# Edge network of a graph kernel: tile sums in two TensorE banks, accumulator written by ScalarE

## What is computed

```
q_i = K_v[dst]
alpha = concat([q_i * K_v[src], q_i * K_E]) * scale
gate = sigmoid(_ln(alpha, ln_g[h], ln_b[h]))
m = concat([V_v[src], V_E])
m = (m @ Wu[h] + bu[h]) * gate
m = _leaky(_ln(m @ Wm[h] + bm[h], mln_g[h], mln_b[h]))
heads.append(segment_sum(m, dst, num_segments=n))
```

## Time and profile before

| what | value |
|---|---|
| median of 3 runs | 13212.4 us (13209.07 to 13218.26) |
| profiled execution | 13231.7 us, span 13229.9 us |
| PE busy | 9252.9 us (70%) |
| DVE busy | 8863.8 us (67%) |
| GpSimd busy | 8813.8 us (67%) |
| ACT busy | 5824.9 us (44%) |
| mean granted TensorE clock | 0.930 of 2.4 GHz |

### The profile page before, as it was taken

One profiled execution on the slowest core, in us unless ns is written; L12 is line 12 of the kernel. 1 busy time (PEld: TensorE's weight loads), 2 busy tenths in 40 slices (PEclk: granted clock), 3 DMA queues, 4 the chain that ended last, 5 costly groups with the idle time before them and its releaser, 6 DMA issues.

```text
span 13229.9 us, 180603 instructions
## 1 busy us (share of the span) xinstructions
PE 9252.9 (70%) x45190; PEld 6129.7 (46%) x45190; DVE 8863.8 (67%) x20382; ACT 5824.9 (44%) x11467; POOL 8813.8 (67%) x6219
## 2 busy tenths in 40 slices
PE   1344444444475888888888888888888888669997
PEld 0233333333223665666666665666666656323322
DVE  3233333333206888888888888888888888327896
ACT  0111111111102666666666666666666666006442
POOL 1588888888603888888888888888888888000000
PEclk9999999999997999989999899999999999889997
DMA  9766666666693443434343344344443343569663
GB/s 413 235 157 150 151 152 151 150 152 153 163 416 109 120 119 119 120 119 120 119 120 119 118 120 120 119 120 119 119 120 120 119 119 110 231 279 359 232 219 125
DMA packets 1232544, 2147.28 MB, mean 162 GB/s; under 512 B 345985, under 2 KB 768210, under 8 KB 1218579
## 3 DMA queue, kind: packets, MB, share of 16 engines
q1 hardware_dynamic: 838120, 1657.69, 36.7%
q0 software_dynamic: 390240, 484.27, 16.9%
q10 hardware_dynamic: 4048, 3.51, 0.1%
HBM read 1652.11 MB, written 492.84 MB: 162 GB/s over the span
## 4 chain that ended last, share of the span: by engine, by line
POOL 44%; issue 20%; PE 15%; DMA 8%; DVE 5%; ACT 3%; SPq 3%; POOLq 1%; DVEq 1%; another core or an unknown queue 0%; ACTq 0%; PEldq 0%
POOL arena L1362 22%; POOL adj L1401 14%; POOL arena L1414 6%; PE psum L1273 5%; DMA arena<-adj 4%; DMA adj<-put_val,put_idx 3%; SPq L1453 3%; PE psum L1318 2%; ACT arena L980 2%; POOL arena L1417 1%; PE psum L1131 1%; PE psum L1285 1%; PE psum L1196 1%; PE psum L1209 1%; PE psum L1186 1%
## 5 line engine op out<-in xcount | busy, mean ns | idle before, releaser
L1401 POOL DMA_INDIRECT adj<-put_val,put_idx x1616 | 2638.3, 1633 | 844.9 <-issue 478.1
L980 ACT ACTIVATE arena<-arena 128x128 f32<-128x128 f32 x6464 | 2657.6, 488 | 298.2 <-DVE arena L774 170.4
L1110 PE MATMUL psum<-ke,arena 64*128 64x256 f32 x3232 | 1451.8, 640 | 1883.2 <-DMA arena<-in_edge_t 1883.2
L1362 POOL DMA_INDIRECT arena<-table1q,idx_dst x1616 | 2249.3, 1392 | 492.6 <-issue 492.6
L1362 POOL DMA_INDIRECT arena<-table,idx_blk x1616 | 1903.5, 1178 | 431.5 <-issue 374.9
L1110 PEld LDWEIGHTS psum<-ke,arena 64*128 64x128 f32 x3232 | 1039.7, 329 | 2294.9 <-issue 2025.9
L1196 PEld LDWEIGHTS psum<-wm,arena 128*128 128x128 f32 x12928 | 1755.6, 203 | 608.0 <-issue 509.4
L986 ACT ACTIVATE arena<-psum,cols 128x512 f32<-128x512 f32 x1616 | 1250.0, 774 | 1710.8 <-PE psum L1178 1386.7
L1186 PE MATMUL psum<-arena,wvu 128*128 128x512 f32 x3232 | 1894.1, 671 | 83.0 <-DVE arena L703 60.2
L1209 PE MATMUL psum<-arena 128*128 128x128 f32 x6464 | 1113.3, 325 | 1119.7 <-DVE arena L730 1107.0
L1196 PE MATMUL psum<-wm,arena 128*128 128x64 f32 x12928 | 1798.2, 285 | 5.9 <-issue 4.6
(11 more groups left out here) (208 smaller groups left out, 11727.7 us busy)
## 6 DMA issues: line engine op xcount, KB each, us to landing
arena<-adj SPq DMA_DIRECT2D x192, 1568.0 KB, 12.5
arena<-adj SPq DMA_DIRECT2D x336, 896.0 KB, 4.7
kept_keys<-arena SPq DMA_DIRECT2D x404, 512.0 KB
arena<-kept_keys SPq DMA_DIRECT2D x404, 512.0 KB
adj<-arena SPq DMA_DIRECT2D x98, 1568.0 KB
arena<-in_edge_t SPq DMA_DIRECT2D x808, 128.0 KB
kept_hot<-arena SPq DMA_DIRECT2D x404, 256.0 KB
arena<-kept_hot SPq DMA_DIRECT2D x404, 256.0 KB
```

Of the source, the lines that this page charges most:

```text
L980: A.activation(to, at_, ACT.Identity, bias=shift[z][:, n:n + 1], scale=rstd[z][:, n:n + 1]).then_inc(normed, 1)
L1110: last = M.matmul(psum[:, 2 + 2 * z + j, t * H * D:(t + 1) * H * D], edge0[z][:, 2 * j + t, :], ke[D:P, :], start=True, stop=True)
L1362: K.indirect_dma_start(out=dst[:, t, :], out_offset=None, in_=table, in_offset=bass.IndirectOffsetOnAxis(ap=idx[:, t:t + 1], axis=0)).then ...
L1401: K.indirect_dma_start(out=adj, out_offset=bass.IndirectOffsetOnAxis(ap=put_idx[s][:, j:j + 1], axis=0), in_=put_val[s][:, j:j + 1], in_of ...
```

## The change

Four tiles of a group are now summed in the same pair of banks (0 and 1, one for each pair of heads). A matmul of zeros opens both banks, and each tile's sums are accumulated at the tile's offset from the group's first destination, which TensorE takes from registers (16 loaded once in four iterations, from a table `offs` made ahead of the stage). ScalarE then writes the group's 512 columns to `acc`: the first column with what is there already as bias, for each pair of heads, the other 511 as a plain copy, since the edges are sorted and nothing else has been written there yet. DVE's four additions and its register loads are gone. `acc` has 384 columns more for each pair of heads. The bias of `o_pair` is one matmul over both tiles, ahead of the wait for the gates. `turn_x` writes bank 7 in place of 0.

```diff
-NW = NP + WIN
+NW = NP + G * WIN
@@ DVE, ahead of the stage
+            link(V.tensor_tensor(offs.rearrange("p (n t) -> p n t", t=G), dst_t[0:1, :].rearrange("p (n t) -> p n t", t=G),
+                                 dst_t[0:1, :].rearrange("p (n t) -> p n t", t=G)[:, :, 0:1].to_broadcast([1, NG, G]),
+                                 ALU.subtract))
@@ DVE, sweep1
-                if now[4] and s == 0:
-                    held[:] = block_bases(DVE, i - 4)
-                regs = held[G * s:G * s + G]
-                def add(t):
-                    if now[4]:
-                        dve.wait_ge(sums1, 2 * (i - 4) + t // 2 + 1)
-                        add_tile(added1, i - 4, t, acc[:, :, bass.ds(regs[t], WIN)],
-                                 psum[:, 1 + 6 * (t // 2), (t % 2) * 2 * WIN:(t % 2 + 1) * 2 * WIN].rearrange(
-                                     "p (j w) -> p j w", j=2))
-                add(0)
-                add(1)
                 if now[1]:
                     gate_m(3)
-                add(2)
-                add(3)
@@ ScalarE, sweep1
+                if now[4] and s == 0:
+                    held[:] = group_bases(ACTE, i - 4)
-                    A.activation(xt[s][0:D].rearrange("p t n -> p (t n)"), psum[0:D, 0, :],
+                    A.activation(xt[s][0:D].rearrange("p t n -> p (t n)"), psum[0:D, 7, :],
                                  ACT.Copy).then_inc(xt_ready, 1)
                 if now[2]:
                     take_o(1)
-            steps(act, sweep1, NG, 4, 2)
+                if now[4]:
+                    act.wait_ge(sums1, 2 * (i - 3))
+                    after(act, added1, 3 * (i - 4))
+                    for half in range(2):
+                        own = acc[:, half, bass.ds(held[s], 1)]
+                        A.activation(own, psum[:, half, 0:1], ACT.Identity, bias=own).then_inc(added1, 1)
+                    A.activation(acc[:, :, 1:NW][:, :, bass.ds(held[s], G * WIN - 1)], psum[:, 0:2, 1:G * WIN],
+                                 ACT.Copy).then_inc(added1, 1)
+            held = []
+            steps(act, sweep1, NG, 8, 4)
@@ TensorE, sweep1
+                if now[4] and s == 0:
+                    held[:] = block_offsets(PE, i - 4)
                 def o_pair(j):
+                    after(pe, o_taken, 2 * (i - 2) + j)
+                    M.matmul(psum[:, 6, :], ones3[:, :], bm_parts[:, :], start=True, stop=False)
                     pe.wait_ge(gm_ready, H * (i - 1))
-                    after(pe, o_taken, 2 * (i - 2) + j)
                     for t in range(2):
                         at_ = t * H * D
                         for h in range(H):
-                            M.matmul(psum[:, 6, at_ + h * D:at_ + (h + 1) * D], gm[z][:, h, 2 * j + t, :],
-                                     wm[:, h, :], start=h == 0, stop=False)
-                        last = M.matmul(psum[:, 6, at_:at_ + H * D], ones3[:, :], bm_parts[:, :],
-                                        start=False, stop=True)
+                            last = M.matmul(psum[:, 6, at_ + h * D:at_ + (h + 1) * D], gm[z][:, h, 2 * j + t, :],
+                                            wm[:, h, :], start=False, stop=t * H + h == 2 * H - 1)
                     last.then_inc(o_done, 1)
+                def clear_sums():
+                    after(pe, added1, 3 * (i - 4))
+                    for half in range(2):
+                        M.matmul(psum[:, half, :], zero_row[0:1, :], zero_row[0:1, 0:1].to_broadcast([1, G * WIN]),
+                                 start=True, stop=False)
                 def sums(j):
                     pe.wait_ge(hot_in[z], 16 * (2 * (k - 1) + s // 2 + 1))
                     pe.wait_ge(msg_ready, i - 3)
-                    after(pe, added1, G * (i - 5) + 2 * j + 2)
                     for t in (2 * j, 2 * j + 1):
                         for half in range(2):
-                            at_ = (t % 2 * 2 + half) * WIN
-                            last = M.matmul(psum[:, 1 + 6 * j, at_:at_ + WIN],
+                            last = M.matmul(psum[:, half, bass.ds(held[G * s + t], WIN)],
                                             msg[z][:, t * H + 2 * half:t * H + 2 * half + 2, :].rearrange("p h d -> p (h d)"),
-                                            onehot[z][:, t, :], start=True, stop=True)
+                                            onehot[z][:, t, :], start=False, stop=t == G - 1)
                 if now[4]:
+                    clear_sums()
                     sums(0)
```

More of the change, by code:

```diff
@@ L25 @@
 PE = mybir.EngineType.PE
+ACTE = mybir.EngineType.Activation
 P = 128
@@ L141, in gnn @@
         vecs = sb("vecs", [D, 6])
-        bm_row = sb("bm_row", [1, H, D])
-        bm_rest = sb("bm_rest", [1, H, D])
-        bm_up = sb("bm_up", [1, H, D])
+        bm_row, bm_rest, bm_up = (acc[0:1, i // 2, NP + i % 2 * H * D:NP + (i % 2 + 1) * H * D].rearrange(
+            "p (h d) -> p h d", h=H) for i in range(3))
+        zero_row = sb("zero_row", [1, P], BF16)
         bm_part = [sb(f"bm_part{i}", [1, H * D], BF16) for i in range(3)]
-        bm_parts = sb("bm_parts", [3, H * D], BF16)
+        bm_parts = sb("bm_parts", [3, 2 * H * D], BF16)
         ones3 = sb("ones3", [3, P], BF16)
@@ L417, in halves_of, with group_bases, block_offsets @@
             return slice(half * HALF + i * CH_N, half * HALF + (i + 1) * CH_N)
-        def block_bases(engine, g):
-            return bases(engine, dst_t[0:1, bass.ds(g * G, U * G)])
+        def group_bases(engine, g):
+            first = dst_t[0:1, bass.ds(g * G, U * G)].rearrange("p (u t) -> p u t", t=G)[:, :, 0]
+            return bases(engine, first)
+        def block_offsets(engine, g):
+            _, regs = nc.values_load_multi_w_load_instructions(
+                offs[0:1, bass.ds(g * G, U * G)], engines=(engine,), min_val=0, max_val=(G - 1) * WIN,
+                skip_runtime_bounds_check_because="every node has an edge, so a tile begins at most a window on")
+            return regs
         @block.vector
@@ L486, in one_hot @@
                     iota_f[:, :].unsqueeze(1).to_broadcast([P, G, WIN]), ALU.is_equal)
-            def add_tile(added, g, t, at_, sums):
-                after(dve, added, g * G + t)
-                V.tensor_tensor(at_, at_, sums, ALU.add).then_inc(added, 1)
             link(V.memset(zeros, 0.0), mark="zeros")
@@ L498, in _ @@
             link(V.memset(ones3[:, :], 1.0))
+            link(V.memset(zero_row[:, :], 0.0))
             dve.wait_ge(s_iota, 4)
@@ L683, in product @@
                                 q[z].unsqueeze(2).to_broadcast([P, G, 2, H * D]), ALU.mult).then_inc(products, 1)
-            held = []
             def sweep1(i, k, s, inside):
@@ L943, in _ @@
             for i in range(3):
-                A.dma_start(bm_parts[i:i + 1, :], bm_part[i][:, :]).then_inc(bm_in, 16)
+                for t in range(2):
+                    A.dma_start(bm_parts[i:i + 1, t * H * D:(t + 1) * H * D], bm_part[i][:, :]).then_inc(bm_in, 16)
             dve_done(f"key_turn{len(TC) - 1}")
@@ L969, in sweep1 @@
             def sweep1(i, k, s, inside):
-                now = [inside or 0 <= i - lag < NG for lag in range(3)]
+                now = [inside or 0 <= i - lag < NG for lag in range(5)]
                 z, odd = s % 2, (s + 1) % 2
+                if now[4] and s == 0:
+                    held[:] = group_bases(ACTE, i - 4)
                 def norm(g, slot, z, h):
@@ L1157, in _ @@
             dve_done("sweep1")
-            pe.wait_ge(bm_in, 48)
+            pe.wait_ge(bm_in, 96)
             def sweep1(i, k, s, inside):
@@ L1235, in sweep1 @@
                     sums(1)
+            held = []
             steps(pe, sweep1, NG, 8, 4)
-            pe.wait_ge(added1, T)
+            pe.wait_ge(added1, 3 * NG)
             for i in range(NBLK):
```

8 lines of the change are left out of this document (5 added, 3 removed).

## The result

The changed kernel took 13171.19 us (median of 7 runs, 13168.37 to 13182.24) beside 13212.55 us for the kernel before on the same chip: a ratio of 0.9970, 95% interval 0.9959 to 0.9982, or 41 us less. The span of the profiled execution is 13168.9 us, 61 us less than before. Of these 61 us, 17 lie in the first eight groups of the stage, where the profiled execution of the kernel before has one group of 33.7 us in place of 15.9; that execution took 19 us more than the median of its kernel. The 390 groups behind them took 6851.9 us before and 6806.1 after, 46 us less, and this is the difference to explain.

A forecast was written before the change was run, and what follows sets the result against it. A DVE and GpSimd ring of 17.55 us per group, times 404 groups, was taken as the bound. Register load -10, one-time work +3 and the end -0.4 gave -7.6 us: forecast 13205 us, range 13185 to 13262.

The forecast's parts named there:

- The ring: Chain from DVE's leaky step to product, then GpSimd's `q` gathers and affine steps to the next leaky step: 17.55 us per group.
- the worth of the additions: DVE's four additions per group, 1.93 us, lie outside the chain that sets the period: removing them gains 0.
- rival (1): DVE binds the stage, so additions and their load come off the period: 711 us less, 12501 us; chance 0.02.
- the sign of a late leaky step: Leaky step L730 starts the chain that sets the period, so its lateness is on the path and costs time.
- a price of 0: Table gathers held up some 0.3 us are absorbed, since the `q` gather waits for the product's end anyway.
- rivals (3) and (4): (3): ScalarE and TensorE bind at gate 1, some 13270 to 13310, chance 0.11; (4): register-load groups late, 13250, chance 0.10.
- nothing either way: On TensorE, one bias matmul of 512 columns replaces two of 256: no gain or loss.
- Rival (2): The period shortens by a changed phase, as the `q` gather's stall varies 0.1 us per group: -40 us, 13165; chance 0.05.
- The register load, -10 us: DVE's load of 16 registers makes the leaky step 0.10 us late in 101 groups; removing it gains 10 us.
- The spare of DVE: DVE's wait for L1417 ahead of the leaky step stays 1.47 us per group, 1.0 in each fourth group.
- The clears: Two clearing matmuls on TensorE, 0.41 us each, are hidden in its 2.77 us wait ahead of `sums(0)`.

The follow-up runs named there:

- e3: Kernel before with DVE's four additions cut from 256 columns to 2 each, most sums left out: 13227.08 us, ratio 1.0001.
- e12: Changed kernel with the old bias of `o_pair`, two matmuls behind the mixing matmuls: 13203.6 against 13200.31 us for the kernel before, ratio 1.0006.
- e15: Kernel before with DVE's register load split, four per group just ahead of the leaky step: 12902.19 against 13200.31 us, ratio 0.9777.
- e13: Kernel before with only the new bias, one 512-column matmul ahead of the gates' wait: 13163.79 against 13200.31 us, ratio 0.9973.
- e16: Kernel before with the bias ahead of the gates' wait as two matmuls of 256 columns: 13189.62 against 13220.79 us, ratio 0.9977.
- e14: Kernel before with only the two clearing matmuls of 512 columns added ahead of `sums(0)`: 13199.05 us, ratio 1.0001.
- e2: Changed kernel with three small DVE memsets ahead of the leaky step: 14001.89 us, ratio 1.0566 to the kernel before.
- e10: Changed kernel with `sums(1)` right behind `sums(0)`, ScalarE's activations behind sigmoid 3, three memsets ahead of the leaky step: 13916.48 us, ratio 1.0519 to the kernel before.
- e17: Changed kernel with the old bias order and three memsets ahead of the leaky step: 13911.14 against 13220.79 us for the kernel before, ratio 1.0534.
- e1: Kernel before with three small DVE memsets between the wait for `affine` and the leaky step: 13023.82 against 13226.1 us, ratio 0.9849.
- e18: Kernel before with registers loaded four at a time ahead of the leaky step and the bias first as one matmul: 12928.73 against 13220.79 us, ratio 0.9779.

## Why the prediction was wrong

**The ring** was right. Its terms are found again in the changed kernel: GpSimd has no releaser ahead of its gathers, 17.6 us in the groups that are on time, and the first `q` gather takes 2.73. So was the worth of the additions: nothing, by e3. In rival (1) the prediction read a rule of the Trainium skill (Perfetto Trace Analysis, Optimizing Scalar/DVE Operations: if DVE is saturated, some work may go to ScalarE) on the busy share, which would have promised 711 us. The page gives no amount. e12, which moves all that work to ScalarE, gains nothing.

**The step that failed** is the sign of a late leaky step. The prediction put a price on lateness ("since L730 starts the ring, this is on the path") and had the fact that refutes it beside it: the first table gather is stalled by the leaky step. It said of this stall only that the `q` gather waits for the product anyway, a price of 0. But a gather that has started is not stalled (in e15, 398 leaky steps start up to 0.28 us into a gather, and these gathers take 1.00 to 1.02 us, not 1.86), so a leaky step that comes 0.35 us later frees 0.85 us of GpSimd. GpSimd then finishes one more `q` gather ahead of the product. That gather counts 1.25 us against a lateness of 0.5. e15 gives the size: 298 us for 0.57 us of lateness. In the changed kernel 89 groups came late and each took 0.6 us less, where the prediction had a late group cost 0.45 to 0.6 us (rivals (3) and (4)). The Trainium skill (SBUF — State Buffer, SBUF: two separate sides) states that of a DVE operation with two SBUF inputs and a GpSimd operation that reads SBUF, the one that starts first holds the shared ports and the other is blocked to its end. The traces agree where DVE starts first (1.86 us). Where the gather starts first they agree that the gather is spared (1.01 us), but DVE is not blocked: the 398 leaky steps of e15 take 1.225 us on the mean, and those of the kernel before 1.226. The prediction had used only the first case.

**The bias, "nothing either way"**, is where the whole gain came in (e12, e13, e16). In the prediction's terms, this term was put at nothing by its work alone. By itself it moves little work: 343.7 us for 808 matmuls against 449.8 for 1616 before, hidden. It lengthens the stretches at 1.2 GHz after TensorE's wait for the leaky step, and late groups follow these. The prediction kept the clock out of the sum. Rival (2) named a changed phase and the size, -40, and then said "Nothing in the change points to it". That sentence was wrong: several edits lay on the way to gate 1, and one of them did it. That its size came out is luck: it took 0.1 us in each group from a stall that varies, and what was measured is 0.6 us in 89 groups and nothing in the others, by a gather more ahead of the product.

**The register load, -10 us**, was not found. Its groups are on time in both kernels, and counted from the trace their periods agree: 17.68 and 17.50 us before and after for the two that lie around the load. The 0.10 us was no lateness of DVE: in the changed kernel, where DVE has no load and waits, the leaky step of that group starts as long after L1431's end (0.14 us).

The changed kernel even has one more such hand-over: in one group in four, 84 in all, the leaky step starts 0.14 us behind L1431's end in place of 0.03 though DVE waits for it, and so 0.20 us behind the index copy. That is still ahead of the first gather, which starts 0.34 us behind the copy, and there lateness does cost what it measures: a period of 17.65 us in place of 17.55, some 8 us in all. It is the prediction's rule, and it holds up to the gather's start. e12 has the same (97 groups, 17.64), so it is not the bias; why the hand-over is longer there is open.

**ScalarE.** The long copy was 1.02 us as reckoned. The small activations took 0.254 each, not 0.20. Four registers cost it 0.89 us, not 0.45 (duration ns min/median/max):

```profile
L395 ACTq TENSOR_LOAD <-dst_t x101: 885/891/1095, 4207.6 to 11186.9; - x101
```

The spare of DVE was judged right on the mean (1.84 us of wait in 305 groups, against 1.45 in 298 before). It was taken to be the same in each group, and it is not: with half-clock stretches of 10 us gate 0 alone waits 4.9 us. Rival (3) had this place, with the price upside down. DVE's busy time fell by 546 us over the whole execution, not 660: the additions' own busy time was 674, but for 125 us of it a neighbour's record ran beside them, so only 549 could go; and the gates took 13 us longer.

**TensorE and once.** The clears took 0.39 us each (0.41 reckoned) and are hidden (e14). The subtraction of the offsets took 1.83 us (1.8).

**Open.** Why a bias matmul ahead of the gates lengthens the half-clock stretches; the runs show only that it does, in the kernel before in two widths (e13, e16) and in the changed one (against e12). Which part of the summing and copying keeps the changed kernel from a period of 16.8 us (e2, e10, e17). What makes the hand-over to the leaky step 0.11 us longer in one group in four of the changed kernel. And that the long stretches make the groups late rests on the order in time: in e13, 55 of the 66 late groups of the whole stage follow one, and the 11 others do not.

## What to carry to other kernels

Where GpSimd's gathers and DVE's operations with two SBUF inputs meet in a ring, ask of each meeting which of the two starts first: half a microsecond of delay on DVE, at the right place, took 298 us (2.3%) off this kernel, more than the change that was meant to relieve DVE. Count the groups of a loop and look at their spread, not at one group, and price "late" by what it collides with. An edit that saves nothing on its engine, such as the place of a bias matmul, can still choose the rhythm; put it in the sum as a range, not as zero.

## What the runs showed of the hardware

- The period as a function of the leaky step's lateness is a sawtooth: 17.57 us at 0.1, 17.65 at 0.2 (the changed kernel), 16.8 from 0.4 to 0.6 (e1, e13, e15), 17.55 at 1.3 (e13), 17.73 at 1.57 (e1), 16.8 again from 1.7 to 1.9 (e18).
- A DVE operation with two SBUF inputs that starts while a gather runs is not held up: 1.225 us for the leaky step, as alone (e15).
- Loading 16 registers took DVE 1.10 us, four took 0.34 (e15); four took ScalarE 0.89 us (the changed kernel).
- An activation of 128x1 took 0.254 us, one of 128x1022 from PSUM 1.02 us (the changed kernel).
- With the bias matmul ahead of the gates' wait, stretches at 1.2 GHz of 10 us or more went from 0 to 90 in the stage (e13), with nearly the same work on TensorE.
